# A graph network's third layer in 128-row tiles: edge attributes summed first, one-hot sums of messages second, block by block

## Chip, cores and metric

One Trainium2 chip, one core of it. The metric is the device time of one execution in microseconds. The kernel before took 7946.03 us, the median of 3 runs (7941.44 to 7952.92).

## What is computed

Four layers over a graph of 6250 nodes and 200000 edges, each behind a layer norm with relu, each added to x. Edges are sorted by dst; dst is drawn so that low nodes get many edges (a uniform number squared), src is uniform. The change lies in the third layer, its sums over edges:

```python
h = relu(layernorm(x))
w = where(src != dst, edge_weight, 0)
x = x + (1 + eps) * h + segment_sum(w[:, None] * h[dst], src)      # third layer
```

The fourth layer needs, among other things, the sum of `edge_attr_64` over the edges of each dst node. It depends on nothing of the third layer, and the kernel computes it beside the third layer's messages. The first layer takes sum, maximum and mean of `edge_attr_32` by src; the second is a graph convolution.

## The kernel before

Stages follow one another, each with a barrier at its end: `prepare_keys`, `count_sources`, `find_ranges`, `rank_and_build` (ranks all edges by src and scatters their rows into `sorted_rows` in that order, building dense slabs of the adjacency on the way), `scan_sorted`, `locate_runs`, `edge_statistics_layer` (first layer), `convolution_layer` (second), `weighted_layer` (third), `gated_layer` (fourth).

A sorted edge e = p * 1600 + j lies on partition p of 125, column j of 1600. `scan_sorted` leaves three arrays in that layout: `same_src` (1 where an edge has the src of the one before), `dst_sorted` and `w_sorted`.

`scan_messages` (L1234) is the stage in question. Ten turns of five steps each handle 32 columns a step. All queues run by semaphores:

- GpSimd (L1283) copies 32 index columns to `gather_index` (L1289) and issues 32 gathers of 125 rows of `feature_table`, 64 floats each (L1294), into one of five `gathered_rows`.
- VectorE first does one dst block of 128 nodes for the attributes: for each visit of 16 tiles of 125 edges, it forms `block_keys` (L1324) and 16 one-hot tiles `block_hot` (L1330), a ring of 16. Then it weights the gathered rows (L1336) and scans 64 columns with `same_src` (L1342), which gives running sums along each partition.
- TensorE multiplies each hot tile with the tile's attributes (L1372) into `block_total`; in float32 one product is two matmul instructions, each with a weight load. SyncE loads the attributes in halves of 8 tiles (L1393), when TensorE has used up the half before.
- ScalarE copies each block's sum to `attr_sum` (L1304).
- SyncE stores the scanned sums; the carries between partitions are worked out at the end.

50 blocks have 131 visits in all, since few tiles meet a late block. The ranges (first and end visit of a block, offset of its tiles) come from `blk_table`, loaded to registers by `load_ranges` (L833). `weighted_layer` then gathers, in `gather_runs` (L708, L710), each node's end row and carry: 98 gathers of 128 rows, and adds them to x (L1446 to L1449). `edge_statistics_layer` uses the same `gather_runs`.

Of the kernel before, what the change touches and what calls it, by code (L numbers as in the profile page):

```python
# [15 lines left out]
P = 128  # L16
# [28 lines left out]
KB = -(-NWIN // P)  # L45
HUGE = 3.0e38
# [515 lines left out]
def scan_sorted(nc, g, sorted_rows, scanned, carries):  # L562
# [8 lines left out]
    with Scope(nc) as s:  # L571
        rows = [s.sb(f"scan_rows{b}", [EP, J, ROW], F32) for b in range(2)]
        out = [s.sb(f"scan_out{b}", [EP, J, 2 * DA], F32) for b in range(2)]
        cap = s.sb("cap", [EP, J], F32)
        differs = s.sb("differs", [EP, J], F32)
# [40 lines left out]
        def _(dve):  # L616
# [3 lines left out]
            for k in range(STEPS):  # L620
                rk, ok = rows[k % 2], out[k % 2]
                same = g["same_src"][:, k * J:(k + 1) * J]
# [5 lines left out]
                nc.vector.tensor_copy(last_key[:, :], src_c[:, J - 1:J])  # L628
                nc.vector.tensor_copy(g["dst_sorted"][:, k * J:(k + 1) * J], dst_c)
# [18 lines left out]
            step(nc.vector.tensor_copy(g["keep_run"][:, :], keep[:, :]))  # L648
# [11 lines left out]
        @block.tensor  # L660
        def _(pe):
            pe.wait_ge(dve_step, 2 + 4 * STEPS)
            nc.tensor.matmul(ps_key[:, :], last_key[:, :].broadcast_to([EP, 2 * DA]), g["ident"][0:EP, 0:EP],
                             start=True, stop=True)
            nc.tensor.transpose(ps_carry[:, :], carry[:, :], g["ident"][0:EP, 0:EP]).then_inc(pe_done, 1)
            pe.wait_ge(shifted, 1)
            nc.tensor.transpose(ps_in[:, :], state[:, :], g["ident"][0:2 * DA, 0:2 * DA]).then_inc(pe_done, 1)

# [276 lines left out]
def edge_statistics_layer(nc, g, scanned, carries, x_in, u, w1, b1, w2, b2):  # L945

    NF = 3 * DA
    with Scope(nc) as s:
# [12 lines left out]
        b2_row = s.sb("b2_row", [P, D], F32)  # L961
        turned = [s.ps(f"feats_turned{b}", [NF, 4, P]) for b in range(2)]
# [15 lines left out]
        OC = -(-HI // 8)  # L978
        x, full = g["x"], (N // P) * P

        @block.sync
        def _(sp):
            sp.dma_start(w1_sb[:, :], w1[0:NF, :]).then_inc(loaded, 16)
# [14 lines left out]
        def _(dve):  # L998
            step = Serial(dve, dve_step)
            step(nc.vector.memset(x[:, N // P, :], 0.0))  # L1000
# [7 lines left out]
                                         ALU.add))  # L1008
            dve.wait_ge(gathered, 16 * 2 * HI)
# [35 lines left out]
        def _(pe):  # L1045
# [6 lines left out]

            pe.wait_ge(feats_ready, 1)
# [22 lines left out]
def kept(nc, ctx, g):  # L1076

    for name, shape, dt in (
# [4 lines left out]
        ("same_src", [EP, NT], F32), ("dst_sorted", [EP, NT], I32), ("w_sorted", [EP, NT], F32),  # L1083
        ("end_i", [P, HI], I32), ("end_part_i", [P, HI], I32), ("has_out", [P, HI], F32), ("spans", [P, HI], F32),
        ("x", [P, HI, D], F32), ("win_table", [1, 2 * NWIN + 2], I32), ("blk_table", [1, 2 * NB + 2], I32),
        ("keep_run", [D, EP], F32),
# [147 lines left out]
def scan_messages(nc, g, table, scanned, carries, edge_attr_64):  # L1234
# [8 lines left out]
    J = NT // NB  # L1243
    STEPS = NT // J
    U = 5
    with Scope(nc) as s:
        index = [s.sb(f"gather_index{b}", [EP, J], I32) for b in range(U)]
        got = [s.sb(f"gathered_rows{b}", [EP, J, D], F32) for b in range(U)]
        out = [s.sb(f"message_sums{b}", [EP, J, D], F32) for b in range(U)]
        carry = s.sb("sum_carry", [EP, D], F32)  # L1250
        state = s.sb("sum_state", [D, EP], F32)
        turned_carry = s.sb("sum_turned_carry", [D, EP], F32)
        carry_in = s.sb("sum_carry_in", [EP, D], F32)
# [4 lines left out]
        iota_f = s.sb("iota_f", [P, P], F32)  # L1258
        total = [s.ps(f"block_total{b}", [P, D + 1]) for b in range(U)]
        ps_carry = s.ps("ps_sum_carry", [D, EP])  # L1260
        ps_in = s.ps("ps_sum_in", [EP, D])
        index_ready = s.sem("index_ready")
        gathered = [s.sem(f"gathered{b}") for b in range(U)]
        weighted = s.sem("weighted")
        scans_done = s.sem("scans_done")
        carry_ready = s.sem("carry_ready")
        sums_out = [s.sem(f"sums_out{b}") for b in range(U)]
        pool_turns = s.sem("pool_turns")
        dve_step = s.sem("dve_step")
        pe_done = s.sem("pe_done")  # L1270
        carried = s.sem("carried")
# [7 lines left out]
        dst_v = scanned[:, :].rearrange("(p j) c -> p (j c)", p=EP)  # L1279
        attr_rows = edge_attr_64.rearrange("(t e) f -> e t f", e=EP)  # L1280

        @block.gpsimd
        def _(pool):  # L1283
            pool.sem_inc(scans_done, U)
            with pool.Fori(0, STEPS // U) as i:
                for b in range(U):

                    pool.wait_ge(scans_done, U * i + b + 1)
                    pool.tensor_copy(index[b][:, :], g["dst_sorted"][:, bass.ds((U * i + b) * J, J)]  # L1289
                                     ).then_inc(index_ready, 1)  # L1290
                    pool.wait_ge(index_ready, U * i + b + 1)
                    pool.sem_inc(pool_turns, 1)
                    for j in range(J):
                        pool.indirect_dma_start(got[b][:, j, :], None, table[:, :],  # L1294
                                                bass.IndirectOffsetOnAxis(ap=index[b][:, j:j + 1], axis=0)
                                                ).then_inc(gathered[b], 16)

        @block.scalar
        def _(act):
            with act.Fori(0, STEPS // U) as i:  # L1300
                before, _ = load_ranges(nc, g["blk_table"], ACTE, i * U, U, MOST)
                for b in range(U):
                    act.wait_ge(used, before[b + 1] * HGRP + HGRP)
                    nc.scalar.copy(g["attr_sum"][:, bass.ds((i * U + b) * (D + 1), D + 1)], total[b][:, :]  # L1304
                                   ).then_inc(copied, 1)

        @block.vector
        def _(dve):
            for b in range(2):
                nc.vector.memset(attr[b][:, :, D:D + 1], 1.0).then_inc(consts, 1)  # L1310
            nc.vector.tensor_copy(iota_f[:, :], g["iota"][:, 0:P]).then_inc(consts, 1)
            nc.vector.tensor_scalar(base[:, :], g["iota"][:, 0:NB], float(P), None, ALU.mult).then_inc(consts, 1)
            nc.vector.memset(carry[:, :], 0.0).then_inc(carry_ready, 1)
            dve.wait_ge(consts, 4)
            dve.sem_inc(made, HGRP)
            with dve.Fori(0, STEPS // U) as i:
                before, offset = load_ranges(nc, g["blk_table"], DVE, i * U, U, MOST)
                for b in range(U):

                    with dve.Fori(before[b], before[b + 1]) as v:  # L1320
                        t = nc.s_assert_within(v * HGRP - offset[b], 0, NT - HGRP,
                                               skip_runtime_bounds_check_because=RANGES)
                        dve.wait_ge(made, v * HGRP + HGRP)
                        nc.vector.tensor_scalar(keys[:, :], g["dkey"][:, bass.ds(t, HGRP)],  # L1324
                                                base[0:EP, bass.ds(i * U + b, 1)], None,
                                                ALU.subtract).then_inc(keys_ready, 1)
                        dve.wait_ge(keys_ready, v + 1)
                        for j in range(HGRP):
                            dve.wait_ge(used, v * HGRP + j + 1)
                            nc.vector.tensor_scalar(hot[:, j, :], iota_f[0:EP, :], keys[:, j:j + 1], None,  # L1330
                                                    ALU.is_equal).then_inc(made, 1)

                    n = U * i + b
                    dve.wait_ge(gathered[b], 16 * J * (i + 1))
                    w = g["w_sorted"][:, bass.ds(n * J, J)]
                    nc.vector.tensor_tensor(got[b][:, :, :], got[b][:, :, :], w.unsqueeze(2).broadcast_to([EP, J, D]),  # L1336
                                            ALU.mult).then_inc(weighted, 1)
                    dve.wait_ge(weighted, n + 1)
                    dve.wait_ge(carry_ready, n + 1)
                    dve.wait_ge(sums_out[b], 32 * i + 1)  # L1340
                    for f in range(D):
                        last = nc.vector.tensor_tensor_scan(out[b][:, :, f], g["same_src"][:, bass.ds(n * J, J)],  # L1342
                                                            got[b][:, :, f], carry[:, f:f + 1], ALU.mult, ALU.add)
                    last.then_inc(scans_done, 1)
                    dve.wait_ge(scans_done, n + 1 + U)
                    nc.vector.tensor_copy(carry[:, :], out[b][:, J - 1, :]).then_inc(carry_ready, 1)
            step = Serial(dve, dve_step)
            dve.wait_ge(pe_done, 1)
            step(nc.vector.tensor_copy(turned_carry[:, :], ps_carry[:, :]))
            step(nc.vector.memset(state[:, 0:1], 0.0))  # L1350

            step(nc.vector.tensor_tensor_scan(state[:, 1:EP], g["keep_run"][:, 0:EP - 1], turned_carry[:, 0:EP - 1],
                                              0.0, ALU.mult, ALU.add))
            dve.wait_ge(pe_done, 2)
            nc.vector.tensor_copy(carry_in[:, :], ps_in[:, :]).then_inc(carried, 1)

        @block.tensor
        def _(pe):
            pe.sem_inc(used, HGRP)
# [442 lines left out]
```

## Time and profile before

| | us |
|---|---|
| median of 3 runs | 7946.03 |
| profiled execution, its span | 7948.8 |
| stage of `scan_messages`, from its first instruction | 4413.0 |
| first and last start of a gather (L1294) | 4414.5, 6949.6 |
| last operation of the third layer (L1449), start | 7112.15 |

| engine | busy us | share |
|---|---|---|
| TensorE matmul | 4702.6 | 59% |
| VectorE | 4461.4 | 56% |
| GpSimd | 4309.1 | 54% |
| TensorE weight load | 3515.5 | 44% |
| ScalarE | 1261.5 | 16% |

The shares are a mean over stages with different limits. What bounds a stage is read from its own stretch: an engine that goes from one instruction to the next with nothing but its own issue between them, while the others wait.

### The profile page before, as it was taken

The page shows a single profiled execution, that of the slowest core. Times are in us where ns is not written, and L with a number is a line of the kernel's source. Part 1 is how long each engine was busy: PE and PEld are TensorE (multiplying, and loading weights), DVE is VectorE, ACT ScalarE, POOL GpSimd, SP SyncE. Part 2 cuts the span into 40 slices and gives each one's busy share as a digit, 9 for nine tenths or more (in the row PEclk, how much of TensorE's full clock was granted, in tenths as well). Part 3 has the DMA queues.
Part 4 walks back from the last instruction along what each step waited for, and adds up shares of the span by engine and source line. Part 5 has one row for each costly group of instructions (what it writes and reads, how often), then busy time and mean ns, then how long its engine had stood idle before and what let it go on. Part 6 is the DMA issues. An engine that isn't in the chain of part 4 may idle for free. (4 is left out here: it accounts for less than half of the span.)

```text
span 7948.8 us, 124234 instructions
## 1 busy us (share of the span) xinstructions
PE 4702.6 (59%) x28437; PEld 3515.5 (44%) x28438; DVE 4461.4 (56%) x14642; ACT 1261.5 (16%) x4005; POOL 4309.1 (54%) x3463
## 2 busy tenths in 40 slices
PE   6589888888888888860038665532222222209696
PEld 5344455555555555540038555432222222208585
DVE  7878666666666666659532667754444444431313
ACT  0023333333333333330000000000000000000101
POOL 0046667666666667660220678777777777740000
PEclk5578867777776777665569555555555555559898
DMA  0001221211221221136527333332222222219191
GB/s 20 1 11 35 59 38 39 59 38 39 57 40 38 39 58 39 37 74 236 162 112 301 70 81 79 83 73 61 61 61 61 57 62 62 57 22 364 43 372 41
DMA packets 612266, 644.26 MB, mean 81 GB/s; under 512 B 396280, under 2 KB 549008, under 8 KB 576519
## 3 DMA queue, kind: packets, MB, share of 16 engines
q1 hardware_dynamic: 471760, 500.71, 20.1%
q0 software_dynamic: 134272, 89.36, 7.5%
q10 hardware_dynamic: 6118, 53.08, 2.0%
q14 instruction: 97, 0.79, 0.0%
q8 instruction: 19, 0.31, 0.0%
HBM read 425.43 MB, written 213.96 MB: 80 GB/s over the span
## 5 line engine op out<-in xcount | busy, mean ns | idle before, releaser
L374 POOL DMA_INDIRECT sorted_rows<-rows,place_i x1600 | 2093.9, 1309 | 1180.0 <-issue 608.7
L1294 POOL DMA_INDIRECT gathered_rows<-feature_table,gather_index x1600 | 2008.1, 1255 | 518.1 <-issue 473.6
L1372 PE MATMUL block_total<-attr_half,block_hot 125*128 125x65 f32 x4192 | 955.9, 421 | 1554.3 <-DMA attr_half<-in_edge_attr_dram 1544.5
L1372 PEld LDWEIGHTS block_total<-attr_half,block_hot 125*128 125x128 f32 x4192 | 912.7, 331 | 1598.4 <-issue 1391.9
L538 PE MATMUL part<-high,low 125*128 x3612 | 1405.3, 528 | 109.6 <-DVE high L414 103.3
L414 DVE TENSOR_TENSOR high<-iota_g,window_keys 125x1568 f16 x903 | 875.2, 969 | 7.4
L1330 DVE TENSOR_SCALAR block_hot<-iota_f,block_keys 125x128 f32<-125x128 f32 x2096 | 604.3, 352 | 425.2 <-PE block_total L1372 264.8
L526 PE MATMUL count_rows<-counts,lo_rows_f 128*125 128x49 f32 x3200 | 761.4, 328 | 0.0
L538 PEld LDWEIGHTS part<-high,low 125*128 x3612 | 436.8, 121 | 683.6 <-issue 613.6
L395 DVE CUSTOM_DVE_ANT_0 picked<-count_rows,oh_hi 125x49 bf16<-125x49 f32 x1600 | 314.0, 235 | 740.8 <-PE count_rows L527 647.7
L526 PEld LDWEIGHTS count_rows<-counts,lo_rows_f 128*125 128x125 f32 x3200 | 673.5, 260 | 92.4 <-issue 87.3
L521 PE MATMUL running<-oh_hi,oh_lo 125*128 125x49 bf16 x1600 | 442.7, 277 | 410.5 <-ACT counts L474 233.4
L1342 DVE TENSOR_TENSOR_SCAN message_sums<-same_src,sum_carry,gathered_rows 125x32 f32<-125x32 f32 x3200 | 608.6, 268 | 7.2 <-DVE gathered_rows L1336 2.3
L474 ACT COPY counts<-running 128x49 f32<-128x49 f32 x1600 | 321.3, 201 | 1806.8 <-PE running L521 1420.4
L521 PEld LDWEIGHTS running<-oh_hi,oh_lo 125*128 125x128 bf16 x1600 | 237.0, 148 | 682.8 <-issue 340.0
L1336 DVE TENSOR_TENSOR gathered_rows<-gathered_rows,w_sorted 125x2048 f32<-125x2048 f32 x50 | 114.8, 2295 | 642.9 <-DMA gathered_rows<-feature_table,gather_index 641.5
L891 PE MATMUL sum_bank_round<-gated_parts,piece_round 128*128 128x193 bf16 x4900 | 426.2, 249 | 47.5 <-DMA piece_round<-slabs 33.7
L891 PEld LDWEIGHTS sum_bank_round<-gated_parts,piece_round 128*128 128x128 bf16 x4900 | 421.0, 98 | 53.0 <-issue 34.3
L409 DVE TENSOR_TENSOR low<-iota_g,lo_tiles 125x512 f16 x903 | 443.6, 491 | 0.0
L527 PE MATMUL count_rows<-oh_hi,earlier 125*125 125x49 bf16 x1600 | 434.3, 271 | 0.0
L407 DVE TENSOR_SCALAR window_keys<-mkeys,winbase x903 | 247.9, 274 | 328.8 <-issue 270.4
L460 ACT CAST slab<-part 128x392 f32 (+1 forms) x800 | 397.5, 501 | 88.5 <-PE part L538 78.7
(343 smaller groups left out, 5496.3 us busy)
## 6 DMA issues: line engine op xcount, KB each, us to landing
piece_round<-slabs SPq DMA_DIRECT2D x140, 1120.0 KB, 7.2
slabs<-slab SPq DMA_DIRECT2D x20, 3920.0 KB, 19.7
piece_conv<-slabs SPq DMA_DIRECT2D x70, 1120.0 KB, 5.2
attr_half<-in_edge_attr_dram SPq DMA_DIRECT2D x262, 250.0 KB
scanned<-scan_out ACTq DMA_DIRECT2D x10, 4480.0 KB
scanned<-message_sums SPq DMA_DIRECT2D x50, 896.0 KB
sorted_rows<-rows,place_i POOLq DMA_INDIRECT x1600
gathered_rows<-feature_table,gather_index POOLq DMA_INDIRECT x1600
```

The costliest lines, as they stand in the source:

```text
L374: pool.indirect_dma_start(sorted_rows[:, :], bass.IndirectOffsetOnAxis(ap=place_i[:, h, u:u + 1], axis=0), rows[:, h, u, :], None).then_in ...
L409: nc.vector.tensor_tensor(low[:, bass.ds(slot * (P * WGRP), P * WGRP)].rearrange("p (a b) -> p a b", b=WGRP), iota_g[0:EP, 0:P, :], g["lo_ ...
L414: nc.vector.tensor_tensor(high[:, bass.ds(slot * (WGRP * KEYW), WGRP * KEYW)].rearrange("p (a b) -> p a b", b=WGRP), iota_g[0:EP, :, :], k ...
L521: nc.tensor.matmul(running[:, :], oh_lo[:, h, :, u], oh_hi[:, h, :, u], start=False, stop=True, skip_group_check=True).then_inc(updated, 1)
L526: nc.tensor.matmul(out, lo_rows_f[:, h, q, v, :], counts[:, u % 2, :], start=True, stop=False)
L527: nc.tensor.matmul(out, earlier[:, h, q, v, :], oh_hi[:, h, :, u], start=False, stop=True).then_inc(count_rows_ready, 1)
L538: last = nc.tensor.matmul(out, low[:, bass.DynSlice(slot * (P * WGRP) + k, P, WGRP)], high[:, bass.DynSlice(slot * (WGRP * KEYW) + k, KEYW ...
L891: last = nc.tensor.matmul(bank[b][:, :], piece[k][:, j, b * P:(b + 1) * P], parts[:, hb, :], start=hb == 0, stop=hb == HI - 1)
L1294: pool.indirect_dma_start(got[b][:, j, :], None, table[:, :], bass.IndirectOffsetOnAxis(ap=index[b][:, j:j + 1], axis=0)).then_inc(gathere ...
L1330: nc.vector.tensor_scalar(hot[:, j, :], iota_f[0:EP, :], keys[:, j:j + 1], None, ALU.is_equal).then_inc(made, 1)
L1342: last = nc.vector.tensor_tensor_scan(out[b][:, :, f], g["same_src"][:, bass.ds(n * J, J)], got[b][:, :, f], carry[:, f:f + 1], ALU.mult, ...
L1372: nc.tensor.matmul(total[b][:, :], hot[:, j, :], attr[j // HALF][:, j % HALF, :], start=False, stop=True, skip_group_check=True).then_inc( ...
```

## The change

Sorted edges are laid out anew for the third layer, in 1568 tiles of 128 consecutive edges (the last ones filled up with edges of weight 0): edge 128 t + p on partition p, column t. A message's product with a one-hot of its src, weighted, sums it to its node within a block of 128 nodes, in PSUM; no scan, no carry and no end rows are needed. Since edges are sorted by src, block i needs only the tiles of its own range.

- `scan_sorted` keeps `src_sorted` too (10 more copies) and drops `keep_run`; `edge_statistics_layer` stores the three sorted arrays to DRAM, loads them with 128 edges as a row, turns them on TensorE and copies them to `src_rows`, `dst_rows`, `w_rows`; it makes `turn_table` (block of the last edge of each group of 16 tiles) and `src_table` (first visit of 4 tiles of each block).
- `sum_messages` replaces `scan_messages`. GpSimd: 98 groups of 16 gathers of 128 rows, in a ring of 8 groups; the table load and the wait at a group's head keep it from overwriting rows not used yet. Group n's rows are announced (`landed`) after the issues of group n + 1.
- TensorE, VectorE and ScalarE go through 49 blocks. In each, all attribute visits come first (16 tiles, as before), then all message visits (4 tiles, hot tiles in four buffers). One PSUM tile for each of the two sums.
- `weighted_layer` adds the sums to x in one operation in place of `gather_runs` and four operations.

The core of the diff (left out are declarations, the key turning in the first layer and the unchanged attribute loops):

```diff
@@ edge_statistics_layer, SyncE, ahead of the loads of weights and x @@
+            for c, name in enumerate(("src_sorted", "dst_sorted", "w_sorted")):
+                two_parts(sp, sorted_keys[c, 0:E].rearrange("(p j) -> p j", p=EP), g[name][:, :], keys_stored)
+            sp.wait_ge(pads_ready, 3)
+            sp.dma_start(sorted_keys[:, E:ST * P].unsqueeze(0), pads[:, :, :]).then_inc(keys_stored, 16)
+            sp.wait_ge(keys_stored, 7 * 16)
...
@@ sum_messages, GpSimd @@
+            pool.iota(iota_n[:, :], pattern=[[1, HI * P]], base=0, channel_multiplier=0,
+                      allow_small_or_imprecise_dtypes=True).then_inc(iota_ready, 1)
+
+            def group(n, r, k, first=False):
+                _, v = nc.values_load_multi_w_load_instructions(g["turn_table"][0:1, bass.ds(n, 1)],
...
+                pool.wait_ge(hot_used, GT * n + VT * (v[0] & 63) + GT + VT)
+                pool.sem_inc(pool_turns, 1)
+                pool.tensor_copy(index[k][:, :], g["dst_rows"][:, bass.ds(n * GT, GT)]).then_inc(index_ready, 1)
+                pool.wait_ge(index_ready, n + 1)
+                pool.sem_inc(pool_turns, 1)
+                for j in range(GT):
+                    pool.indirect_dma_start(got[:, (k * GT + j) * D:(k * GT + j + 1) * D], None, table[:, :],
+                                            bass.IndirectOffsetOnAxis(ap=index[k][:, j:j + 1], axis=0)
+                                            ).then_inc(gathered[k], 16)
+                if k:
+                    pool.wait_ge(gathered[k - 1], LANDED * (r + 1))
...
+                pool.sem_inc(landed, 1)
...
@@ sum_messages, VectorE, in each block after the attribute visits @@
+                first, last = visits(DVE, i)
+                with dve.Fori(first, last + 1) as q:
+                    t = nc.s_assert_within(q * VT, 0, ST - VT, skip_runtime_bounds_check_because=RANGES)
+                    v = q + i
+                    for j in range(VT):
+                        dve.wait_ge(hot_used, v * VT + FREE - VT + j + 1)
+                        nc.vector.tensor_scalar(hot_src[j][:, :], iota_n[:, bass.ds(i * P, P)],
+                                                g["src_rows"][:, bass.ds(t + j, 1)], g["w_rows"][:, bass.ds(t + j, 1)],
+                                                ALU.is_equal, ALU.mult).then_inc(hot_ready, 1)
@@ sum_messages, TensorE, in each block after the attribute visits @@
+                first, last = visits(PE, i)
+                pe.wait_ge(agg_copied, i + 1)
+                nc.tensor.matmul(ps_agg[:, :], g["zerob"][:, 0:P], g["zerob"][:, 0:D], start=True, stop=True)
+                with pe.Fori(first, last + 1) as q:
+                    v = q + i
+                    pe.wait_ge(landed, (q >> 2) + 2)
+                    for j in range(VT):
+                        pe.wait_ge(hot_ready, v * VT + j + 1)
+                        nc.tensor.matmul(ps_agg[:, :], hot_src[j][:, :],
+                                         got[:, bass.ds(((q & (RING * GT // VT - 1)) * VT + j) * D, D)], start=False, stop=True,
+                                         skip_group_check=True).then_inc(hot_used, 1)
```

with GT = 16, RING = 8, VT = 4, ST = 1568 tiles and FREE = 132. `visits(engine, i)` loads two values of `src_table` (a sorted edge's number divided by 512) to registers.

## Rows read from the trace of the kernel before

**Rows 1.** The page's slices of the span, 40 equal parts of 198.7 us each.
```profile
POOL 0046667666666667660220678777777777740000
PEclk5578867777776777665569555555555555559898
```
**Rows 2.** Instruction groups, 4380 to 7200 us: xcount | busy, mean ns | idle before.
```profile
L1294 POOL DMA_INDIRECT gathered_rows<-feature_table,gather_index x1600 | 2008.1, 1255 | 518.1 <-issue 473.6 <-POOL gather_index L1289 44.5
L1372 PE MATMUL block_total<-attr_half,block_hot 125*128 125x65 f32 x4192 | 955.9, 421 | 1554.3 <-DMA attr_half<-in_edge_attr_dram 1544.5 <-DVE block_hot L1330 5.1 <-issue 3.3
L1330 DVE TENSOR_SCALAR block_hot<-iota_f,block_keys 125x128 f32<-125x128 f32 x2096 | 604.3, 352 | 425.2 <-PE block_total L1372 264.8 <-issue 36.9 <-DVE block_keys L1324 2.8
```
**Rows 3.** Waits, 4413 to 6974 us: total us, times, longest.
```profile
PE block_total L1372 <- DMA attr_half<-in_edge_attr_dram: 1544.5, 194, 44.2
```
**Rows 4.** Timeline of GpSimd at a change of group: start, us taken.
```profile
4714.17 0.22 POOL L1289 COPY gather_index<-dst_sorted 125x32 int32 x1
4715.29 1.27 POOL L1294 DMA_INDIRECT gathered_rows<-feature_table,gather_index  x1 [0.90 <-POOL gather_index L1289]
```
**Rows 5.** Gathers by line: ns min/median/max, first and last start.
```profile
L1294 POOL DMA_INDIRECT gathered_rows<-feature_table,gather_index x1600: 1205/1209/3309, 4414.5 to 6949.6; - x178
...
L708 POOL DMA_INDIRECT ends<-scanned,end_i x49: 940/944/982, 3908.7 to 4031.7; - x49
```
**Rows 6.** Timeline: a gather beside L1336, and gathers of end rows.
```profile
4725.91 2.37 DVE L1336 TENSOR_TENSOR gathered_rows<-gathered_rows,w_sorted 125x2048 f32<-125x2048 f32 x1
...
4727.47 1.89 POOL L1294 DMA_INDIRECT gathered_rows<-feature_table,gather_index  x1 [0.30 <-issue]
...
7000.26 0.94 POOL L708 DMA_INDIRECT message_ends<-scanned,end_i  x1 [0.30 <-issue]
...
7028.97 0.94 POOL L710 DMA_INDIRECT message_carry<-carries,end_part_i  x1 [0.30 <-issue]
```
**Rows 7.** Timeline of TensorE in block 0, eight tiles a row.
```profile
4420.46 3.67 PE L1372 MATMUL block_total<-attr_half,block_hot 125*128 125x65 f32 x16 [5.68 <-DMA attr_half<-in_edge_attr_dram]
...
4429.36 3.67 PE L1372 MATMUL block_total<-attr_half,block_hot 125*128 125x65 f32 x16 [1.32 <-DMA attr_half<-in_edge_attr_dram]
```
**Rows 8.** Timeline of VectorE: 16 hot tiles, 8 of them, keys after a turn.
```profile
4415.38 3.61 DVE L1330 TENSOR_SCALAR block_hot<-iota_f,block_keys 125x128 f32<-125x128 f32 x16
...
4421.18 3.27 DVE L1330 TENSOR_SCALAR block_hot<-iota_f,block_keys 125x128 f32<-125x128 f32 x8 [1.76 <-PE block_total L1372]
...
4799.10 0.24 DVE L1324 TENSOR_SCALAR block_keys<-dkey,block_base 125x16 f32 x1 [7.30 <-issue]
```
**Rows 9.** Register work and table loads by line: ns min/median/max.
```profile
L407 DVEq FUSED_REGOPS  x1761: 4/186/209, 370.4 to 3534.7; - x196
...
L538 PEldq FUSED_REGOPS  x3612: 74/74/88, 372.3 to 3537.1; - x191
...
L833 DVEq TENSOR_LOAD <-blk_table x10: 859/2624/3748, 4413.7 to 6716.3; - x10
```
**Rows 10.** Stretches, L1324 alone (one per visit): us, busy (count), clock, DMA.
```profile
4413.00:4545.00 132.00, 4.30 (x15) 0.50 0.36 77
...
5160.00:6974.00 1814.00, 29.28 (x70) 0.50 0.27 62
```
**Rows 11.** Timeline of VectorE at the stage's end and the layer's.
```profile
6952.66 2.29 DVE L1336 TENSOR_TENSOR gathered_rows<-gathered_rows,w_sorted 125x2048 f32<-125x2048 f32 x1 [31.52 <-DMA gathered_rows<-feature_table,gather_index]
...
7112.15 3.42 DVE L1449 TENSOR_TENSOR x<-x,message_ends 128x3136 f32<-128x3136 f32 x1
```
**Rows 12.** Timeline of VectorE in the first layer.
```profile
3922.20 0.22 DVE L1005 SCALAR_TENSOR_TENSOR bias<-w_u,u_col,bias 128x1 f32<-128x1 f32 x1 [13.08 <-DMA x<-in_x_dram]
...
4035.91 3.42 DVE L1012 TENSOR_TENSOR run_carry<-run_carry,spans 128x3136 f32<-128x3136 f32 x1 [110.16 <-DMA run_carry<-carries,end_part_i]
```
**Rows 13.** The costs of an iota and of a copied key column, by line.
```profile
L751 POOL IOTA tile_count_i<- x1: 1462/1462/1462, 276.1 to 276.1; 128x1600 int32 x1
...
L629 DVE CAST dst_sorted<-scan_rows x10: 293/296/300, 3577.8 to 3853.7; 125x160 int32<-125x160 f32 x10
```

More of the change, by code:

```diff
@@ L45 @@
 KB = -(-NWIN // P)
+GT = 16
+SG = 2 * HI
+ST = SG * GT
+SBLK = -(-ST // P)
+STAIL = ST - (SBLK - 1) * P
+DUMMY = HI * P - 1
+RING = 8
+VT = 4
 HUGE = 3.0e38
@@ L621, in _ @@
                 rk, ok = rows[k % 2], out[k % 2]
[L622 removed]
+                same = same_src[:, :]
                 dve.wait_ge(rows_in[k % 2], 32 * (k // 2 + 1))
@@ L1298, in _ @@
+            for k in range(RING):
+                group(k, 0, k, True)
+            with pool.Fori(1, SG // RING) as r:
+                for k in range(RING):
+                    group(r * RING + k, r, k)
+            for k in range(SG % RING):
+                group(SG - SG % RING + k, SG // RING, k)
+            pool.wait_ge(gathered[SG % RING - 1], LANDED * (SG // RING + 1))
+            pool.sem_inc(landed, 1)
         @block.scalar
         def _(act):
[L1300 to L1305, printed above, removed]
+            with act.Fori(0, HI) as i:
+                before, _ = load_ranges(nc, g["blk_table"], ACTE, i, 1, MOST)
+                act.wait_ge(used, before[1] * HGRP + HGRP)
+                nc.scalar.copy(g["attr_sum"][:, bass.ds(i * (D + 1), D + 1)], total[:, :]).then_inc(copied, 1)
+                v = visits(ACTE, i)
+                act.wait_ge(hot_used, (v[1] + i + 1) * VT + FREE)
+                nc.scalar.copy(agg[:, bass.ds(i * D, D)], ps_agg[:, :]).then_inc(agg_copied, 1)
@@ L1310, in _ @@
                 nc.vector.memset(attr[b][:, :, D:D + 1], 1.0).then_inc(consts, 1)
-            nc.vector.tensor_copy(iota_f[:, :], g["iota"][:, 0:P]).then_inc(consts, 1)
             nc.vector.tensor_scalar(base[:, :], g["iota"][:, 0:NB], float(P), None, ALU.mult).then_inc(consts, 1)
-            nc.vector.memset(carry[:, :], 0.0).then_inc(carry_ready, 1)
-            dve.wait_ge(consts, 4)
+            dve.wait_ge(consts, 3)
+            dve.wait_ge(iota_ready, 1)
             dve.sem_inc(made, HGRP)
[L1316 to L1355, printed above, removed]
+            with dve.Fori(0, HI) as i:
+                before, offset = load_ranges(nc, g["blk_table"], DVE, i, 1, MOST)
+                with dve.Fori(before[0], before[1]) as v:
+                    t = nc.s_assert_within(v * HGRP - offset[0], 0, NT - HGRP, skip_runtime_bounds_check_because=RANGES)
+                    dve.wait_ge(made, v * HGRP + HGRP)
+                    nc.vector.tensor_scalar(keys[:, :], g["dkey"][:, bass.ds(t, HGRP)], base[0:EP, bass.ds(i, 1)], None,
+                                            ALU.subtract).then_inc(keys_ready, 1)
+                    dve.wait_ge(keys_ready, v + 1)
+                    for j in range(HGRP):
+                        dve.wait_ge(used, v * HGRP + j + 1)
+                        nc.vector.tensor_scalar(hot[:, j, :], iota_n[0:EP, 0:P], keys[:, j:j + 1], None, ALU.is_equal
+                                                ).then_inc(made, 1)
+                first, last = visits(DVE, i)
[7 more added lines that the diff above has]
+                                                ALU.is_equal, ALU.mult).then_inc(hot_ready, 1)
@@ L1398, in _ @@
-            for b in range(U):
-                sp.wait_ge(sums_out[b], 32 * STEPS // U + 1)
-            sp.wait_ge(carried, 1)
-            sp.dma_start(carries[:, :], carry_in[:, :]).then_inc(sums_out[0], 16)
-            sp.wait_ge(sums_out[0], 32 * STEPS // U + 17)
-def weighted_layer(nc, g, table, scanned, carries, eps, edge_attr_64):
+            with sp.Fori(0, HI) as i:
+                before, offset = load_ranges(nc, g["blk_table"], SPE, i, 1, MOST)
+                with sp.Fori(before[0], before[1]) as v:
+                    t = nc.s_assert_within(v * HGRP - offset[0], 0, NT - HGRP, skip_runtime_bounds_check_because=RANGES)
+                    for k in range(2):
+                        sp.wait_ge(used, v * HGRP + (k + 1) * HALF)
+                        sp.dma_start(attr[k][:, :, 0:D], attr_rows[:, bass.ds(t + k * HALF, HALF), :]
+                                     ).then_inc(attr_in[k], 16)
@@ L1440, in _ @@
                 step = Serial(dve, dve_step)
+                step(nc.vector.tensor_tensor(x[:, :, :], x[:, :, :], agg[:, :].rearrange("p (b f) -> p b f", f=D), ALU.add))
                 dve.wait_ge(loaded, 16)
```

206 lines of the change are left out of this document (116 added, 90 removed).

## Prediction

> **What bounds the kernel now.** I read the page's slices first, for the place: from 4413 us on, GpSimd is the busiest engine and TensorE's clock is granted at 0.5 [rows 1]. This is the second layer from the end, with scan_messages. Then the groups of that stage: 1600 gathers of 1255 ns on GpSimd, 2008 us busy with only issue before them, against 956 us of TensorE and 604 us for VectorE's hot tiles [rows 2]. The waits confirm it: TensorE waits 1544.5 us for halves of attributes, and GpSimd for its own issue and copies alone [rows 2, 3]. Last its timeline: a gather of 1.21 us [rows 5], 0.30 us of issue [rows 6], the next one: a pitch of 1.51 us, and at a change of group (copy 0.22 us, then 0.90 us) 0.83 us more (4714.17 to 4715.29, less the usual 0.30) [rows 4]. 1600 x 1.51 + 50 x 0.83 = 2458 us, of the 2536 us from the first gather's start (4414.5) to the last one's end (6949.6 + 1.21) [rows 5]. The other 78 us are gathers held up; the one of 1.89 us stands beside the weighting tensor_tensor L1336 [rows 6]. So this stage is as long as its gathers. The attribute halves that TensorE seems to wait for cost nothing now.
>
> **GpSimd after the change.** 98 groups of 16 gathers of 128 rows in place of 1600 of 125 rows. A gather of 128 rows stands in the trace: those of the ends and carries, 49 of L708 between 940 and 982 ns, median 944 [rows 5], with 0.30 us before each [rows 6]: from 7000.26 to 7028.97 there are 23 pitches of 1.248 us. Index column, 256-byte rows and queue are alike; what differs from the 1209 ns of L1294 is the number of rows. I take 1.248 us; the other bound is 1.51 us. A group change costs 0.83 us as before; added are a table load, register work and a wait for landed rows. GpSimd's queue may run ahead of its engine, so I take these at nothing, with an upper bound from VectorE's loads of blk_table, 0.86 to 3.75 us [rows 9]. Hot tiles are built by tensor_scalar beside gathers today, and the median gather stays at 1209 ns [rows 5], so 0.1 us per group is enough for them. Group: 16 x 1.248 + 0.83 + 0.1 = 20.9 us; 98 of them 2048 us. L1336 and the scans of L1342 go, with their hold-ups.
>
> Here a rule speaks against the change: by the Trainium skill (SBUF — State Buffer, Who interferes with whom), tensor_scalar can enter a mode in which VectorE locks GpSimd out for the whole instruction. Were each of the 1756 new hot tiles to cost GpSimd its 0.226 us, the stage would be 397 us longer. The trace disagrees: L1330 is a tensor_scalar too, 2096 times, and the median gather has no such price [rows 2, 5]; L1336, with two inputs in SBUF, has one [rows 6].
>
> **TensorE and VectorE after the change.** These now work on one block at a time: all attribute visits, then all message visits.
> Attribute visit (16 tiles): eight tiles in 3.67 us, and the same half is back 8.9 us after its start (4420.46 to 4429.36) [rows 7]. Half a visit of work and a round trip of 5.2 us of the transfer set the rhythm, and that wait comes onto the path. The gathers get denser, so I take 9.0 us. The first visit of a block finds both halves loaded: 2.1 us less per block. Visits by block, from the counts of L1324 [rows 10]: 15 in block 0, then 11 in two blocks, 12 in three, 21 in the next seven (23 with block 13's two), then two each: 131.
> Message visit (4 tiles): 200000 / 512 = 391 visits, and one more for each of 49 boundaries less one: 439, some 9 per block. TensorE needs 4 x 0.459 = 1.84 us at this clock [rows 7]. VectorE makes an unhindered hot tile in 3.61 / 16 = 0.226 us [rows 8]. Its new instruction has three addresses from registers. L407, of the same sort, takes 186 ns of register work; TensorE's address in L538 takes 74 ns [rows 9]. Hidden behind the running instructions the visit costs 1.84 us, not hidden 4 x (0.459 + 0.186 + 0.074) = 2.9 us. I take 2.1 us, near the hidden end, because the register instruction of each attribute tile is also hidden in those 3.67 us.
> Block change: two short table loads (0.86 us for twelve values, [rows 9]; two and four now), keys and the first hot tile before TensorE can go on. I take 2.5 us. The bounds are 0.9 us and the 7.30 us that VectorE stands idle at the turn of today's five-block loop, before the keys at 4799.10 [rows 8].
> By another rule (Runtime: NRT & Kernel Launch, Instruction fetch mechanics) of the Trainium skill, a taken branch to a target outside the fetched pages stalls the engine; with 7.3 us at each of 49 turns instead of 10 this is part of rival C. The trace has only the 7.30 us, of a body with five blocks and 320 scans; the new body has one block and some 20 vector instructions, so I do not expect it.
>
> **The sum of the stage.** GpSimd may be eight groups (128 tiles, four blocks) ahead. Late blocks: 2 x 9.0 - 2.1 + 9 x 2.1 + 2.5 = 37 us against GpSimd's 42 us for 32 tiles, so GpSimd bounds. Early blocks: block 0 needs 154 us and blocks 3 to 5 each 55 us, so GpSimd runs into the end of its ring and waits. Start: GpSimd first makes an iota of 6272 columns, at L751's 1462 ns for 1600 columns 5.7 us [rows 13]; with the first copy 8 us. Blocks 0 to 12: 59 x 9.0 - 13 x 2.1 = 504, messages 13 x 9 x 2.1 = 246, changes 33: 791 us. Group 34 can start when group 26 is used up, which needs block 13's attributes and three visits: 15.9 + 2.5 + 6.3 = 25, so 816 us. From there 64 groups x 20.9 = 1338: 2154 us. The last landing and five visits add 12 us: 2166 us. GpSimd alone would have been done in 2068; the early blocks cost about 100 us.
> Now: from 4413.0 the stage with what follows it lasts to 7112.15 + 3.42 = 7115.6, 2702.6 us [rows 11]. That includes the last weighting and scan (6952.66 on), the carries, 98 gathers of end rows and five tensor operations of 3.4 us. All that goes but two of the tensor operations: 2166 + 10 = 2176 us. Gain 527 us.
>
> **Elsewhere.** scan_sorted gets ten copies of src_sorted, like L629 (296 ns, overlapping: 0.21 us each) [rows 13]: +2 us on VectorE, which sets that stage. The first layer gets seven stores, six loads and 43 TensorE operations to turn the sorted keys. All the stores and loads stand ahead of the weights and x on SP's queue, with two waits: x, needed at 3922 today, comes later, and VectorE's addition of b2 and 16 copies behind it. All this is hidden as long as it ends before the end rows: VectorE idles 110 us for them, until 4035.9 [rows 12]. 2.4 MB there and back in 512-byte pieces, by the 13 us that VectorE waits for x's load (1.5 MB in 256-byte pieces) some 40 us, turns and copies 30: 40 us of cover remain. Without that cover it would cost what exceeds 110 us.
> Sum: 7948.8 - 527 + 2 = 7424 us. The profiled execution's 7948.8 lies 2.8 over the median, so 7421 us; in short 5255 + stage.
>
> **Rivals.**
> A: 128 rows cost as much as 125. Group 25.1 us, stage 98 x 25.1 + 20 = 2480: 7735 us. Against it stand 98 equal rows [rows 5].
> B: The table load, its wait and the landing wait at each group are not hidden: +1.9 us per group (half of the worst load). Group 22.8, and the early waits shrink to some 35 us: 2288, so 7543 us.
> C: TensorE and VectorE become the bound throughout, if a message visit costs over 2.4 us or a block change over 7. Stage 8 + 131 x 9.0 - 49 x 2.1 + 439 v + 49 c. With v = 3.0 and c = 2.5: 2523, so 7778. With v = 2.1 and c = 9.8: 2486, so 7741. With v = 2.6: 2347, so 7602.
> E, slower than before: only four hot tiles are buffered, so VectorE and TensorE could take turns instead of overlapping: 4 x 0.41 for VectorE at its hindered pace (3.27 us for eight [rows 8]), 1.84 for TensorE and 0.75 for the two loops: 4.2 us. Stage 8 + 1076 + 439 x 4.2 + 122 = 3050: 8305 us. From 3.4 us per visit on it is slower. Against it: a ring of 16 shows no such turns, and four tiles cover a hand-over of 1.2 us.
> That the change does not do what it says is A or C in another form; no further case.
>
> **Chances.** Forecast (7350 to 7500) 0.52; A 0.07; B 0.14; C 0.13; D 0.09; E 0.05. The range reaches from D to C's near end, 7320 to 7620, and leaves out A, E, and C's larger half: under 2 in 10. A measurement of this kernel tells about 0.2% (16 us) from no change. Faster 0.94, within it 0.01, slower 0.05.
>
> **What would show it.** Gathers of 128 rows at 0.94 us in the sum stage; GpSimd gaps of under 2 us at group changes; waits of GpSimd for TensorE's hot tiles in the first 800 us and none later; about 2.1 us from one message visit to the next; the next layer's first tensor operation some 2180 us after 4413; VectorE's wait for end rows in the first layer still there. Wrong would be the forecast if late blocks, too, took over 42 us, or if GpSimd's pitch stayed at 1.5 us.

## The result, and the profile after

The changed kernel took 8886.94 us (median of 4 runs, 8883.86 to 8902.43) against 7943.73 us for the kernel before (4 runs, 7925.15 to 7952.92): 1.1195 times as long, 95% interval 1.1177 to 1.1213. The forecast was 7421 us. The runs below showed later that this holds under one of two conditions; under the other the same kernel took 7214 us against 7805 us (one run each).

Of the page of the changed kernel, two slices (40 equal parts of 222 us), then three groups (xcount | busy, mean ns | idle before):

```profile
span 8882.2 us, 143063 instructions
POOL 0056766676676666030143344444444444430000
PEclk5588777776686667558755555555555555557988
L1459 PE MATMUL ps_agg<-gathered_rows,hot_src 128*128 x3512 | 906.2, 430 | 1371.8 <-issue 1203.4
L1375 POOL DMA_INDIRECT gathered_rows<-feature_table,gather_index x1568 | 1484.6, 947 | 526.2 <-issue 487.1
L1430 DVE TENSOR_SCALAR hot_src<-iota_n,src_rows,w_rows 128x128 f32 x1756 | 572.5, 352 | 2034.2 <-remote 991.2
```

GpSimd, at 7 tenths all through the stage in [rows 1], is now at 3 to 4. Its gathers are as short as forecast (947 ns against the 1255 of [rows 2]), and TensorE and VectorE have no more work than the sum gave them: 3512 passes are 1756 tiles. But both stand idle before it, TensorE mostly for "issue" and VectorE for about half of the time for "remote", that is for nothing that another engine's work explains. The waits of the stage, 4440 to 8100 us (total us, times, longest):

```profile
POOL gather_index L1371 <- PE ps_agg L1459: 1491.2, 48, 124.4
...
PE ps_agg L1459 <- issue: 1203.4, 382, 7.1
DVE hot_src L1430 <- remote: 991.2, 244, 5.4
```

GpSimd, which bounded the stage before [rows 2], waits for used buffers at 48 group changes. TensorE's timeline in one block (start, us taken, passes, idle before):

```profile
6484.81 8.88 PE L1459 MATMUL ps_agg<-gathered_rows,hot_src 128*128 x38
6494.34 0.69 PE L1459 MATMUL ps_agg<-gathered_rows,hot_src 128*128 x2 [0.65 <-issue]
6498.04 0.66 PE L1459 MATMUL ps_agg<-gathered_rows,hot_src 128*128 x2 [3.01 <-issue]
6500.15 0.66 PE L1459 MATMUL ps_agg<-gathered_rows,hot_src 128*128 x2 [1.46 <-issue]
6502.89 0.69 PE L1459 MATMUL ps_agg<-gathered_rows,hot_src 128*128 x2 [2.08 <-issue]
6507.88 0.69 PE L1459 MATMUL ps_agg<-gathered_rows,hot_src 128*128 x2 [4.30 <-issue]
...
6529.59 0.69 PE L1459 MATMUL ps_agg<-gathered_rows,hot_src 128*128 x2 [4.91 <-issue]
6534.00 3.73 PE L1459 MATMUL ps_agg<-gathered_rows,hot_src 128*128 x16 [3.72 <-DVE hot_src L1430]
```

Nineteen tiles in a row at 0.47 us each, nearly five visits in 8.9 us, as forecast. Then one tile (two passes) every 2 to 7 us, and from 6534 full pace again. GpSimd's timeline of the same block has its first and its last gather where the slow part lies:

```profile
6487.98 0.97 POOL L1375 DMA_INDIRECT gathered_rows<-feature_table,gather_index  x1 [0.78 <-POOL gather_index L1371]
...
6527.46 0.94 POOL L1375 DMA_INDIRECT gathered_rows<-feature_table,gather_index  x1 [0.30 <-issue]
```

The loop's register instructions, by line (ns min/median/max), show the same from the inside (PEldq is the sequencer that issues TensorE's instructions):

```profile
L1454 PEldq ALU_OP  x1366: 3/36/1404, 4677.0 to 8035.1; - x196
L1454 PEldq COMPARE_BRANCH  x439: 3/212/1421, 4678.7 to 8035.2; - x147
```

An addition of 36 ns can take 1.4 us. Counted over the records, 887 of TensorE's register instructions took over 280 ns, nine in ten of them 500 to 735 (median 700, longest 1437), all in this stage; in the kernel before none did. VectorE had 199, all but two in this stage, in its attribute loop too. SyncE had 36, 12 of them in this stage; in the kernel before it had 25. GpSimd's gathers come in 49 bursts, most of 32. Each of the 1084 slow register instructions that TensorE and VectorE had in the stage lies between 3.9 us after a burst's first gather and 4.1 us after the end of its last.

The first burst, of 128 gathers beside the attribute visits of block 0, has none of these. There SyncE, which loads the attributes, has ten, and TensorE waits for a half 25 us once and 41 us three times:

```profile
4480.62 3.67 PE L1449 MATMUL block_total<-attr_half,block_hot 125*128 125x65 f32 x16 [41.23 <-DMA attr_half<-in_edge_attr_dram]
```

From the iota to its first message visit block 0 took 289 us, where the prediction's terms give about 141. The question was now: is it the gathers, the waits, or the loop?

### The profile page after: what moved, and what is told of

Same layout as the page of the kernel before. It is cut to its first block and busy times, and to the rows that moved or that the text cites. A ratio compares the mean times of both kernels' runs of the same rounds, so it can differ in the third digit from the quotient of the medians.

```text
span 8882.2 us, 143063 instructions
## 1 busy us (share of the span) xinstructions
PE 5604.8 (63%) x32010; PEld 4323.5 (49%) x32011; DVE 4163.1 (47%) x13105; ACT 1274.0 (14%) x4053; POOL 3704.2 (42%) x3383
## 5 line engine op out<-in xcount | busy, mean ns | idle before, releaser
L1459 PE MATMUL ps_agg<-gathered_rows,hot_src 128*128 x3512 | 906.2, 430 | 1371.8 <-issue 1203.4
L1375 POOL DMA_INDIRECT gathered_rows<-feature_table,gather_index x1568 | 1484.6, 947 | 526.2 <-issue 487.1
L1430 DVE TENSOR_SCALAR hot_src<-iota_n,src_rows,w_rows 128x128 f32 x1756 | 572.5, 352 | 2034.2 <-remote 991.2
L1459 PEld LDWEIGHTS ps_agg<-gathered_rows,hot_src 128*128 128x128 f32 x3512 | 802.8, 325 | 1469.3 <-issue 1462.5
L1449 PE MATMUL block_total<-attr_half,block_hot 125*128 125x65 f32 x4160 | 935.9, 420 | 378.7 <-DMA attr_half<-in_edge_attr_dram 249.3
L1422 DVE TENSOR_SCALAR block_hot<-iota_n,block_keys 125x128 f32<-125x128 f32 x2080 | 484.5, 284 | 394.9 <-remote 131.6
L1371 POOL COPY gather_index<-dst_rows 128x16 int32 (+1 forms) x98 | 19.4, 198 | 1512.5 <-PE ps_agg L1459 1491.2
```

Of the source, the lines that this page charges most:

```text
L1375: pool.indirect_dma_start(got[:, (k * GT + j) * D:(k * GT + j + 1) * D], None, table[:, :], bass.IndirectOffsetOnAxis(ap=index[k][:, j:j + ...
L1422: nc.vector.tensor_scalar(hot[:, j, :], iota_n[0:EP, 0:P], keys[:, j:j + 1], None, ALU.is_equal).then_inc(made, 1)
L1430: nc.vector.tensor_scalar(hot_src[j][:, :], iota_n[:, bass.ds(i * P, P)], g["src_rows"][:, bass.ds(t + j, 1)], g["w_rows"][:, bass.ds(t + ...
L1449: nc.tensor.matmul(total[:, :], hot[:, j, :], attr[j // HALF][:, j % HALF, :], start=False, stop=True, skip_group_check=True).then_inc(use ...
L1459: nc.tensor.matmul(ps_agg[:, :], hot_src[j][:, :], got[:, bass.ds(((q & (RING * GT // VT - 1)) * VT + j) * D, D)], start=False, stop=True, ...
```

## The experiments

Theories: **G128**, gathers of 128 rows do it; **GANY**, any gather beside these loops; **WAIT**, ScalarE and GpSimd waiting on the semaphore that TensorE posts for each tile; **LOOP**, the loop with its register work. Lines of the kernels after an edit are one to three higher.

**First series: four edits.** The runs of a series were made one after another on one chip, each kernel once unless said, with the kernel before beside them.

```
e1_rows125            indirect_dma_start(got[0:EP, ...], ..., ap=index[k][0:EP, j:j + 1])
e2_before_rows128     (before) index, got: [EP, ...] -> [P, ...], index set to 0 once; readers use 0:EP
e3_no_gathers         indirect_dma_start(...) x 16 -> pool.sem_inc(gathered[k], 16 * GT)
e4_scalar_waits_once  act.wait_ge(hot_used, (v[1] + i + 1) * VT + FREE) -> act.wait_ge(summed, i + 1)
                      pe, per block: + wait_ge(hot_used, (last + i + 1) * VT + FREE); sem_inc(summed, 1)
```

> The changed kernel, each gather cut to 125 rows as the kernel before has it (the last 3 edges of each tile are left out of the sums). In the trace of the changed kernel the register instructions of TensorE and VectorE (32 to 73 ns as a rule) take 700 or 1400 ns in stretches that begin some 4.5 us after the gathers of a block begin and end within 4 us of their end. Theory G128: it is the gather of 128 rows that does it, since 125-row gathers ran beside such instructions all through the kernel before and none was slow; then these stretches go, the stage falls from about 3600 us to 2200 to 2500, and the kernel takes 7450 to 7750 us. Theory GANY (any gather beside this loop), theory WAIT (ScalarE and GpSimd waiting on the semaphore that TensorE posts for every tile) and theory LOOP (the loop itself): within 1% of 8887 us.

> The kernel before with each gather of its second layer made 128 rows (three rows more that nothing reads; the outputs stay as they were). Theory G128: register instructions of TensorE and VectorE become slow here too, the turn of 32 gathers and its scans becomes longer, and the kernel takes 8100 us or more. The other theories: each gather takes 0.95 us in place of 1.21 at the same pitch of 1.25, no register instruction is slow, and the kernel takes 7944 us within 0.5%.

> The changed kernel without its gathers: the rows are zero, each group only posts what its gathers would (so the weighted sum of neighbours is left out of the result). GpSimd waits for the free buffers just as before. Theories G128 and GANY: no register instruction is slow, message visits take 1.8 to 2.1 us, the stage takes 2000 to 2200 us and the kernel 7200 to 7450 us. Theories WAIT and LOOP: the slow stretches stay, and the kernel takes over 8600 us.

> The changed kernel, with ScalarE's wait for the messages of a block moved from the semaphore that TensorE posts for every tile (against a register's value) to one that TensorE posts once for each block. Theory WAIT: the slow stretches go and the kernel takes 7400 to 7700 us. Theories G128, GANY and LOOP: within 1% of 8887 us.

Measured: 7592, 7392, 7015 and 7227 us, and no register instruction over 280 ns in any. The last three lie below every range given for them: those had been worked out from a kernel before of 7944 us, and that of e2 from an equal pitch of 1.25 us for both kinds of gather, where the 125-row one has 1.51 [rows 4 to 6]. It looked like a verdict for WAIT, but 125-row gathers with ScalarE's wait left in place had none either, and the kernel before took 7796 us beside them, not 7944. So the changed kernel itself had to be run beside one of them.

**Second series: the changed kernel unaltered.**

> The changed kernel unaltered, on the chip of this call, since the four runs above (125-row gathers, the kernel before with 128-row gathers, no gathers, ScalarE waiting once for each block) had none of the slow register instructions, and the kernel before took 7796 us there and not 7944. Theory WAIT (ScalarE's wait on the semaphore posted for every tile, together with 128-row gathers): slow stretches in the trace, and 8700 to 8950 us. Theory CHIP (the slow stretches belong to the chip or the moment of the first measurement, not to the program): no register instruction over 280 ns in the stage, and 7200 to 7450 us.

> The kernel in which ScalarE waits once for each block, again, beside the changed kernel on the same chip. Theory WAIT: about 1500 us less than the changed kernel. Theory CHIP: within 1% of the changed kernel, both 7200 to 7450 us.

Here the kernel before took 7946.5 us, the changed one 8891.0 (4 runs; ratio 1.1188, 1.1164 to 1.1212) and the one whose ScalarE waits once 8956.4, with 819 slow register instructions on TensorE: the very kernel that had taken 7227. WAIT falls. The two series had run on two chips by their numbers (7 and 11).

**Third and fourth series.** They repeated e1, e2 and e3, and again met the other condition: kernel before 7791 and 7805 us, 125 rows (e7, e12) 7581 and 7577, before with 128 rows (e9) 7389, no gathers (e8) 7000. One new edit (e10) took three of TensorE's 14 register instructions and three waits out of each message visit (a single wait for the four hot tiles): 7324 us. And the changed kernel, unaltered, at last under this condition:

> The changed kernel unaltered. Theory CHIP (the slow register instructions come on one kind of chip only, that on which the kernel before takes 7946 us): beside a kernel before of 7791 to 7796 us it takes 7200 to 7300 us with no slow register instruction; beside one of 7946 us it takes 8891 us again. If it takes over 8600 us beside a kernel before of 7796 us, the slow stretches belong to the program, and the other runs were spared by their edits.

It took 7214.0 us beside a kernel before of 7805.1 us, 7.6% less. The same lines as above, from its page, its waits (4300 to 6600 us), its register instructions and its timeline:

```profile
span 7212.3 us, 143063 instructions
L1459 PE MATMUL ps_agg<-gathered_rows,hot_src 128*128 x3512 | 813.8, 427 | 199.1 <-POOLq L1382 197.0
...
POOL gather_index L1371 <- PE ps_agg L1459: 59.5, 7, 28.9
...
L1454 PEldq ALU_OP  x1366: 32/36/36, 4387.5 to 6367.4; - x196
...
5641.83 9.42 PE L1459 MATMUL ps_agg<-gathered_rows,hot_src 128*128 x40
5659.06 7.37 PE L1459 MATMUL ps_agg<-gathered_rows,hot_src 128*128 x32 [7.81 <-POOLq L1382]
```

No register instruction is slow, and TensorE waits for landed rows (POOLq L1382): GpSimd bounds late blocks, as forecast. Call the two conditions kind S (slow register instructions) and kind F. The slow stretches belong to the program and the condition together.

Two kinds of chip are not shown, though the expectations speak of them. Chip number 11 was S in the second series and F in the fourth; whether one number is always one chip is not known, so S and F may also be two states of a chip. The traces do show where the kernel before loses its 2%. In `rank_and_build`, whose 125-row scatters run beside busy engines too, the last scatter starts 3367 to 3392 us into each F trace and 3520 to 3567 us into each S trace; the stages from there to the gathers last about as long in both.

**Fifth series, on kind S (kernel before 7928.9 us).**

> The changed kernel with gathers of 125 rows (the last 3 edges of each tile are left out). Beside a kernel before of 7946 us: theory G128 gives no slow register instruction and 7500 to 7800 us, theory GANY gives 8850 to 9100 us with slow stretches. Beside one of 7800 us: 7580 us, as in its other runs.

> The kernel before with gathers of 128 rows. Beside a kernel before of 7946 us: theory G128 gives slow register instructions of TensorE and VectorE in the last layer, and over 7800 us; theory GANY gives none and 7500 to 7650 us. Beside one of 7800 us: 7390 us, as in its other runs.

> The changed kernel, with TensorE waiting once for each message visit (11 register instructions in place of 14). Beside a kernel before of 7946 us: if each register instruction beside a gather can be slow by itself, 100 to 250 us less than 8891 us; if the slow ones are as many per microsecond whatever TensorE runs, within 1% of 8891 us. Beside one of 7800 us: 7324 us, as in its first run.

Measured: 7746.6, 8785.2 and 8761.3 us. With 125 rows TensorE has 50 slow register instructions and not 887 (VectorE 55, SyncE 59), and the kernel is 2.3% faster than the one before. As the loop is the same, LOOP falls too (without gathers the kernel was never run on kind S). And the kernel before, given 128-row gathers, loses 856 us without any part of the change: both times of GANY fail, both of G128 hold. Two things of G128 did not come true: 125-row gathers leave some slow register instructions, so they disturb less rather than not at all, and in e14 no register instruction of TensorE or VectorE is slow in the stage. There SyncE is hit, which issues the attribute halves. Waits of its stage, first on kind S, 4450 to 7800 us:

```profile
PE block_total L1375 <- DMA attr_half<-in_edge_attr_dram: 2047.0, 152, 41.5
DVE block_hot L1333 <- remote: 1074.2, 282, 6.1
SPq L1396 <- remote: 1737.2, 85, 42.1
```

then the same kernel on kind F, 4250 to 6600 us, where SyncE has no such wait at all:

```profile
PE block_total L1375 <- DMA attr_half<-in_edge_attr_dram: 1161.0, 190, 35.7
```

An engine's stream of instructions stands still or creeps while the gathers run, and which engine is hit most differs from kernel to kernel. With a single wait per visit (e15), TensorE's message loop is free of slow register instructions; 122 are left in its attribute loop and at block changes, and VectorE has 344 in place of 199. 130 us come back against 8891, but that is a kernel of another series (1.105 times the kernel before in place of 1.119), and on kind F the same edit costs 110 us (7324 against 7214). So the theory's number held and its reason did not: many of the slow instructions moved rather than went. Between the kinds this kernel still differs by 1437 us (8761 and 7324). Thinning this loop out is no cure.

**Sixth series, with a kernel before of 7863.4 us: pace or form.** A 125-row gather comes every 1.51 us, a 128-row one every 1.25. Their form differs as well: counted over the packets of the gathers' queue, a 128-row gather moves its rows in 16 packets of 2048 bytes (8 rows each), a 125-row one in 5 shares of 25 rows, each a packet of 4096 and one of 2304 bytes. With the small packets that is 32 against 48.

```
e16_paced_gathers   + pool.memset(spare[j][:, :], 0.0)  behind each gather, spare[j]: [P, P]
e17_rows112         indirect_dma_start(got[0:112, ...], ..., ap=index[k][0:112, j:j + 1])
e18_paced_1500      as e16, spare[j]: [P, 3 * P]
```

> The changed kernel with a memset of a spare 128x128 tile on GpSimd (about 0.2 us) behind each 128-row gather, so that the gathers come at a pitch of 1.45 to 1.75 us in place of 1.25. Beside a kernel before of about 7940 us: theory PACE gives next to no slow register instruction and 7650 to 8050 us; theory FORM gives slow stretches as long as before or longer (the same gathers, further apart) and 8800 to 9500 us. Beside one of about 7800 us: both give 7500 to 7850 us.

> The changed kernel with gathers of 112 rows, seven for each of 16 DMA engines (the last 16 edges of each tile are left out). Beside a kernel before of about 7940 us: theory FORM gives slow stretches and over 8500 us; theory PACE gives, by the pitch that its trace shows, over 8500 us if it is 1.25 us or less and 7500 to 7800 us if it is about 1.5 us. Beside one of about 7800 us: 7200 to 7590 us, and only the pitch is learned.

Measured: 8608.7 and 8811.0 us. Gathers as their timelines show them, first e16, then e17:

```profile
6311.01 0.22 POOL L1379 MEMSET spare<- 128x128 f32 x1
6311.39 0.95 POOL L1376 DMA_INDIRECT gathered_rows<-feature_table,gather_index  x1 [0.16 <-issue]
```

```profile
6431.31 0.94 POOL L1377 DMA_INDIRECT gathered_rows<-feature_table,gather_index  x1 [0.30 <-issue]
6432.56 0.94 POOL L1377 DMA_INDIRECT gathered_rows<-feature_table,gather_index  x1 [0.30 <-issue]
```

The issue gap shrank from 0.30 us to 0.16, so the pitch became 1.33 us and not the 1.45 or more expected; 410 register instructions of TensorE stayed slow. So some 7% more pitch halved their number, which the form alone doesn't explain, but the time lies between the two theories' ranges, and this run didn't reach the pitch where they part. 112 rows are as fast (pitch 1.24) and as harmful (907 slow) as 128: it isn't the number 128, nor the bytes. They do come in the same form, 16 packets of 1792 bytes, and at the same pace, so this run can't part the two theories. The condition here is a third one, between S and F by the kernel before and by the last scatter (3447 and 3462 us), yet e17's stage is as slow as on kind S.

**Seventh series: a pitch of 1.54 us.**

> The changed kernel with a memset of 384 columns (0.43 us) behind each 128-row gather: pitch 0.95 + 0.43 + 0.16 = 1.54 us, about that of the 125-row gathers. Theory PACE: fewer than 100 slow register instructions of TensorE; 7700 to 7850 us beside a kernel before of 7930 to 7950 us, 1 to 3% less than it, and 7580 to 7680 us beside one of 7800 us. Theory FORM (an even number of rows for each DMA engine, with the pace as a smaller influence): over 250 slow ones and over 8200 us beside a kernel before of 7860 us or more; beside one of 7800 us it can't be told from PACE.

It met kind F: 7652.4 us (4 runs) against 7800.9, ratio 0.9816 (0.9800 to 0.9833), pitch 1.55 us where 1.54 was worked out. Pace against form stays open. The slow register instructions of TensorE outside kind F are 887 at a pitch of 1.25 us, 907 at 1.24 (112 rows), 410 at 1.33 and 50 at 1.51. The second and third come from the sixth series; the last comes with the other form, so it isn't a clean fourth point.

## Why the prediction was wrong, point by point

**The bound before** (gathers set the stage): right. e9, the kernel before with nothing but shorter gathers, took 402 us less than it on kind F (7389 against 7791, one run each; 1600 x 0.26 = 416 by the pitches).

**GpSimd after**: right on both kinds in its own terms. 944 ns median, pitch 1.25 us, 0.78 us from copy to gather. On kind F 154 gathers with their group changes took 199.9 us (5600.5 to 5800.4), 20.8 us for 16, where the sum had 20.9. Rivals A and B are out; so is D, for the granted clock was 0.50 over the whole stage on both kinds. The rule weighed there, from the Trainium skill's page SBUF — State Buffer (Who interferes with whom), would have shown as longer gathers beside 1756 tensor_scalar tiles; means of 947 ns (S) and 952 ns (F) leave no room for its 0.226 us a tile.

**Message visit, 2.1 us**: twenty tiles in 9.42 us on kind F are 1.9 us a visit; with four hot tiles VectorE and TensorE do overlap, so E's mechanism did not occur. The other terms came out smaller too: attribute visits took about 8.6 us for 9.0, and TensorE was over a block change in 0.6 to 1.5 us for 2.5, so that blocks in which it caught up with GpSimd took 33 us for 37. On kind S the undisturbed stretches are the same; in the disturbed one shown, four tiles take from 6494.34 to 6507.88, 13.5 us.

**The sum of the stage, 2176 us**: on kind F from the iota (4254.0) to the end of L1509 (6375.3 + 3.5) it is 2124.8 us, 2.4% under the sum, and the kernel gained 591 us where 525 were forecast. On kind S the same from 4389.7 to 8043.9 is 3654 us, 1478 over. That is the whole miss: 8882 less the 7424 of the sum is 1458, since the stage began 25 us sooner than the sum had it. Of the 1529 us between the two kinds 154 fall to block 0, where SyncE is slow (289 and 135 us), the rest to the blocks after it.

**Elsewhere**: right. VectorE still waits for the end rows behind all the turned keys, though on kind S with 24 us to spare, not 40 (on kind F 79):

```profile
4013.49 3.42 DVE L1075 TENSOR_TENSOR run_carry<-run_carry,spans 128x3136 f32<-128x3136 f32 x1 [23.89 <-DMA run_carry<-carries,end_part_i]
```

**The step that failed** is the one that made the gathers denser and costed the density with 0.1 us per attribute visit and nothing else: "The gathers get denser, so I take 9.0 us". On kind S what the 128-row gathers do to the other engines is the largest term, some 1500 us: with 125 rows in their place the kernel took 7747 us, and the kernel before lost 856 us by them alone. Whether it is their density or their form is open. The 128-row gathers from which I took the 944 ns, 98 in a row each time [rows 5, 6], stand beside nearly idle engines, so their rows couldn't show it; and a price for the neighbours had no bound in the range. None of the rivals named it. The outcome lies nearest to C (TensorE and VectorE bound), and C's condition did come true, a visit above 2.4 us, but not by C's reasons: neither register work left unhidden in general nor block changes. The second of the Trainium skill's rules that were weighed (Runtime: NRT & Kernel Launch, Instruction fetch mechanics), a stall at a taken branch to instructions not at hand, can't be the whole either: the instructions that take long are additions as well as branches, and on kind F the same loops have none.

**What would have shown it wrong** was named rightly: on kind S most late blocks took 68 to 70 us against a limit of 42, and GpSimd waited for TensorE long after the first 800 us.

Open: what on kind S carries a gather's disturbance into another engine's instruction stream, whether pace alone cures it there, and what makes a run S or F. What tells them apart is the time of the kernel before (7929 to 7947 us on S, 7791 to 7805 on F) and, in each trace, the length of `rank_and_build`.

## What to carry to other kernels

When a change makes a source of small indirect gathers faster, look for what its neighbours do while it runs, and look in a stretch where they are busy; a duration read beside idle engines prices the gather, not the company. Slow register instructions (a median of 36 ns with a maximum of 1400) beside "issue" and "remote" waits are the sign. And before an edit is credited with a gain, run the unedited kernel beside it, in the same series: the 1730 us between e4 (7227) and e6 (8956), one and the same kernel, would have passed for the worth of an edit.

## What the runs showed of the hardware

- A 128-row gather takes 944 ns on GpSimd and a 112-row one 937, a 125-row one 1209 (medians); pitch 1.25, 1.24 and 1.51 us. The first two move their rows in 16 packets, the last in 5 shares of 25 rows (two packets each); that this sets the time is not shown.
- On kind S, gathers of 128 and 112 rows at a pitch of about 1.25 us slow other engines' instruction streams: single register instructions of mostly 700 and up to 1437 ns in place of some 36, stretches in which SyncE issues nothing for up to 42 us (e14). The kernel before is 2% slower under this condition, the dense-gather kernels 19% (e14: 8785 against 7389) and 23% (the changed one: 8891 against 7214).
- Which engine is hit depends on the kernel and the stretch: TensorE most in the changed one (SyncE in its block 0), VectorE with fewer waits on TensorE (e15), SyncE in the scan kernel (e14).
- The disturbance starts and ends some 4 us behind the gathers: 3.9 us or more after a burst's first, 4.1 us at most after the end of its last.
